# Level products of the last layer's scan: right rows of two tiles packed in one bank, then placed and added by 0/1 products

## What is computed

```python
z = zxbcdt[..., :HID]                       # HID = 512
dt = jax.nn.softplus(dt_raw + dt_bias)
a = (dt * A).reshape(Bsz, nc, Q, H)         # Q = 128 tokens, H = 64 heads
cum = jnp.cumsum(a, axis=2)
diff = cum[:, :, :, None, :] - cum[:, :, None, :, :]
Lmat = jnp.exp(jnp.where(tril, diff, -jnp.inf))
CB = jnp.einsum('bcihn,bcjhn->bcijh', Cc, Bc)
M = CB * Lmat * dtc[:, :, None, :, :]
Yd = jnp.einsum('bcijh,bcjhp->bcihp', M, xs_c)
...
y = (Yd + Yoff).reshape(Bsz, L, H, P) + D[None, None, :, None] * xs
yz = y * (z * jax.nn.sigmoid(z))
yn = yz * rsqrt(mean(yz * yz) + EPS) * norm_w
return yn @ W_out.T
```

## Time and profile before

| | us |
|---|---|
| median of 3 runs | 1101.43 |
| lowest, highest | 1097.45, 1101.68 |
| the profiled execution's own time | 1101.78 |
| its span, first to last instruction | 1100.0 |

### The profile page before, as it was taken

The page is one execution under the profiler, slowest core; times in us unless marked ns, Lnnn a source line. Parts: engine busy times, 40 slices in busy tenths (PEclk is TensorE's granted clock), DMA queues, the critical chain, the costliest instruction groups (busy, mean ns, idle before and its releaser), DMA issues. The chain is left out here.

```text
span 1100.0 us, 12854 instructions
## 1 busy us (share of the span) xinstructions
PE 958.4 (87%) x4126; PEld 497.6 (45%) x4130; DVE 784.6 (71%) x1393; ACT 463.8 (42%) x768; POOL 465.6 (42%) x479
## 2 busy tenths in 40 slices
PE   5998899799999998789999888887888788878887
PEld 2776555233333333445555554344433553364325
DVE  3768465788878886477767457975799469948895
ACT  3332153267666667455554345221621261125311
POOL 2220365554444440263373305930295118710881
PEclk9999699799999999999999978998999899989999
DMA  8500053222222200300000010000000000000000
GB/s 296 205 15 15 15 160 127 68 58 60 59 59 59 59 2 1 136 1 15 15 1 15 1 41 1 1 1 20 0 0 0 20 0 0 0 20 0 0 0 19
DMA packets 28653, 43.11 MB, mean 39 GB/s; under 512 B 6480, under 2 KB 21792, under 8 KB 28192
## 3 DMA queue, kind: packets, MB, share of 16 engines
q1 hardware_dynamic: 28592, 42.41, 12.4%
HBM read 30.93 MB, written 11.27 MB: 38 GB/s over the span
## 5 line engine op out<-in xcount | busy, mean ns | idle before, releaser
L1102 DVE TENSOR_REDUCE l_nmax<-banks 128x1 f32<-128x512 f32 (+1 forms) x165 | 147.8, 930 | 34.9 <-PE banks L1211 33.6
L1057 ACT ACTIVATE l1b_PT<-banks 128x512 f32<-128x512 f32 (+1 forms) x176 | 134.1, 793 | 66.8 <-PE banks L1224 66.4
L2442 PE MATMUL banks<-l_scaled,l_cbm 128*128 128x512 f32 x224 | 126.3, 681 | 39.6 <-POOL l_scaled L2153 21.8
L2153 POOL TENSOR_TENSOR l_scaled<-l_X,l_source 128x512 f32<-128x512 f32 x112 | 134.5, 1226 | 0.0
L2321 DVE TENSOR_TENSOR banks<-banks,l_decay 128x512 f32<-128x512 f32 x128 | 88.1, 691 | 12.4 <-PE banks L2442 8.0
L2442 PEld LDWEIGHTS banks<-l_scaled,l_cbm 128*128 128x128 f32 x224 | 40.9, 207 | 112.1 <-POOL l_scaled L2153 80.4
L1211 PE MATMUL banks<-l_KQ 96*128 96x512 bf16 x240 | 81.3, 392 | 8.5 <-DVE l_nmax L1102 5.6
L2295 DVE TENSOR_TENSOR l_y<-l_y,banks 128x512 f32<-128x512 f32 x128 | 86.7, 677 | 1.9
L1224 PE MATMUL banks<-l_KQ 99*128 99x512 bf16 x256 | 85.2, 386 | 2.9 <-ACT l1b_PT L1057 2.1
L2222 ACT ACTIVATE l_hhi<-l_h 128x512 f16<-128x512 f32 (+1 forms) x24 | 15.1, 630 | 136.2 <-DVE l_h L2334 136.2
L2140 POOL TENSOR_TENSOR l_across<-l_X,l_source 128x512 f32<-128x512 f32 x16 | 17.0, 1074 | 121.9 <-ACT l_X L2208 121.9
(11 more groups left out here) (332 smaller groups left out, 2040.9 us busy)
## 6 DMA issues: line engine op xcount, KB each, us to landing
l_split<-l1a_parts SPq DMA_DIRECT2D x16, 384.0 KB, 3.3
l_KQ<-l_split SPq DMA_DIRECT2D x48, 128.0 KB, 2.9
l_KQ<-l_split SPq DMA_DIRECT2D x16, 192.0 KB, 3.1
l_KQ<-l_split SPq DMA_DIRECT2D x48, 64.0 KB, 2.8
w_ternary<-l_tern_out SPq DMA_DIRECT2D x7, 384.0 KB, 2.3
x<-in_x SPq DMA_DIRECT2D x4, 512.0 KB, 9.5
l_raw<-in_w_gate_up SPq DMA_DIRECT2D x2, 1024.0 KB, 10.1
out<-x SPq DMA_DIRECT2D x4, 512.0 KB, 3.0
```

Source lines behind the costliest of these rows:

```text
L1057: nc.scalar.activation(PT[:, first:first + size, :], source, ACT.Exp, scale=SCALE).then_inc(p_ready, 1)
L1102: nc.vector.tensor_reduce(nmax[:, H % 2, first:first + size], source, axis=AX.X, op=ALU.max, negate=True).then_inc(smax_read, 1)
L2153: nc.gpsimd.tensor_tensor(by_head(scaled[:, n % 4, :]), by_head(X[:, T, :]), spread(source[:, level, T, :]), ALU.mult).then_inc(scaled_rea ...
L2442: last = nc.tensor.matmul(bank, cbm[:, T % 2, level, :], scaled[:, own_n % 4, :], start=True, stop=True)
```

## The change

Only rows of right halves of a level's product are not zero: 64 of 128. The kernel after keeps these rows alone and packs two tiles in one bank.

- `cbm` becomes 128x64 for a level and tile (`right_columns` picks the right tokens' columns). It is made by seven instructions of 64 columns for a tile instead of one of 896, tiles 0 and 1 before the first product and tiles 2 and 3 later.
- A unit is a level of a pair of tiles. Its two products (64 output rows each) go to the lower and upper half of one bank by `tile_position`. There are 14 units and four across products, in `ITEMS`; they take turns in banks 4 and 5.
- DVE decays the whole bank once for a unit and writes the result to `decayed` in SBUF (ring of three). The decays of the packed rows are new: 14 small products with `prefix` and one exponential on ACT (`right_decay`).
- PE places the rows: for each unit two products with 64 source rows and a 128-wide 0/1 matrix (`place`), which add up over the seven levels in bank 6 and bank 7. DVE adds each of these banks to `y` once for a tile (`take_placed`).
- `y` = X times `coef` (`start`) and `hlo` (`rest_of_gated`) move from POOL to DVE. The hidden products stand at other places, the first of them ahead of the first product.
- DVE's order is written out call by call.

```diff
+                    if n == 4:
+                        act.wait_ge(sums_made, b * 3 + 3)
+                        nc.scalar.activation(right_decay[:, :, :, :].rearrange("p l t h -> p (l t h)"),
+                                             k.pair(0).rearrange("p n s -> p (n s)")[:, 0:LEVELS * 2 * L3_HEADS],
+                                             ACT.Exp).then_inc(decay_ready, 1)
...
+                    for level in range(LEVELS):
+                        half = 1 << level
+                        last = nc.vector.tensor_tensor(cbm[:, T, level, :].rearrange("p (b h) -> p b h", h=half),
+                                                       right_columns(diagonal, level),
+                                                       w.masks[:, level, :].rearrange("p (b h) -> p b h", h=half), ALU.mult)
...
+                    if T is None:
+                        u = UNIT.index(n)
+                        if u == 0:
+                            dve.wait_ge(decay_ready, b * 3 + 3)
+                        if u >= 3:
+                            dve.wait_ge(placed, b * OWN + (u - 2))
+                        nc.vector.tensor_tensor(by_head(decayed[:, u % 3, :]), by_head(bank),
+                                                spread(right_decay[:, level, pair, :]), ALU.mult).then_inc(bank_read, 1)
...
+                    nc.vector.tensor_tensor(y[:, T, :], y[:, T, :], ps[6 + T % 2][:, :], ALU.add).then_inc(y_taken, 1)
...
+                take_decayed(5)
+                mask(2)
+                rest_of_gated(1)
+                take_decayed(6)
+                gated(2)
+                mask(3)
+                take_decayed(7)
...
+                take_decayed(14)
+                take_decayed(15)
+                gated(5)
+                take_decayed(16)
+                take_placed(2, 15)
+                weigh(2)
+                rest_of_gated(5)
+                take_decayed(17)
+                take_placed(3, 17)
+                weigh(3)
...
+                pe.wait_ge(decay_ready, b * 3 + 1)
+                for level in range(LEVELS):
+                    for m in range(2):
+                        rows = slice(m * RIGHT, (m + 1) * RIGHT)
+                        columns = slice(level % 4 * 2 * L3_HEADS, (level % 4 + 1) * 2 * L3_HEADS)
+                        last = nc.tensor.matmul(ps[level // 4][rows, columns], w.prefix[:, level, :],
+                                                a[:, m::2, :], start=True, stop=True, tile_position=(0, m * RIGHT))
...
+                        for m in range(2):
+                            rows = slice(m * RIGHT, (m + 1) * RIGHT)
+                            last = nc.tensor.matmul(bank[rows, :], cbm[:, 2 * pair + m, level, :], scaled[:, (2 * u + m) % 4, :],
+                                                    start=True, stop=True, tile_position=(0, m * RIGHT))
...
+                    for m in range(2):
+                        rows = slice(m * RIGHT, (m + 1) * RIGHT)
+                        last = nc.tensor.matmul(ps[6 + m][:, :], w.place[rows, level, :], decayed[rows, u % 3, :],
+                                                start=(level == 0), stop=(level == LEVELS - 1))
...
+                for n in range(NI + 2):
+                    if n < NI:
+                        product(n)
+                        for j in range(FT):
+                            if HIDDEN_AT[j] == n:
+                                hidden(b, j)
+                    if n >= 2 and ITEMS[n - 2][2] is None:
+                        place(n - 2)
```

More of the change, by code:

```diff
@@ L1885, with right_half, right_columns @@
 PREFIX, SUFFIX = LEVELS, LEVELS + 1
+RIGHT = P // 2
+def right_half(level):
+    k, half = np.arange(RIGHT), 1 << level
+    return k // half * 2 * half + half + k % half
+def right_columns(ap, level):
+    return ap.rearrange("p (b two h) -> p b two h", two=2, h=1 << level)[:, :, 1, :]
 def weights3(k, aps, loaded):
@@ L1911, in layout3 @@
     tok = np.arange(P)
-    masks, sums = [], []
+    masks, sums, places = [], [], []
     for level in range(LEVELS):
@@ new lines, in _ @@
+                for u in range(OWN):
+                    pair, level = divmod(u, LEVELS)
+                    for m in range(2):
+                        T = 2 * pair + m
+                        if level == 0:
+                            pool.wait_ge(xtok_ready, b * TT + (T + 1))
+                        if u >= 2:
+                            pool.wait_ge(prod_made, b * NI + (UNIT[u - 2] + 1))
+                        nc.gpsimd.tensor_tensor(by_head(scaled[:, (2 * u + m) % 4, :]), by_head(X[:, T, :]),
@@ L2307, in _, with rest_of_gated @@
+                def rest_of_gated(j):
+                    rows = P if j < FT - 1 else LAST
+                    dve.wait_ge(hhi_ready, b * FT + (j + 1))
+                    nc.vector.tensor_tensor(hlo[0:rows, j, :], h[0:rows, j % 2, :], hhi[0:rows, j, :],
+                                            ALU.subtract).then_inc(hsplit, 1)
+                for T in range(2):
+                    dve.wait_ge(cb_ready, b * TT + (T + 1))
+                    mask(T)
                 dve.wait_ge(cb_ready, b * TT + TT)
@@ new lines, in product, with place @@
+                    last.then_inc(prod_made, 1)
+                def place(n):
+                    pair, level, _ = ITEMS[n]
+                    u = UNIT.index(n)
+                    pe.wait_ge(bank_read, b * NI + (n + 1))
+                    if level == 0:
+                        if pair:
+                            pe.wait_ge(y_taken, b * TT + 2)
+                        else:
+                            pe.wait_ge(cb_ready, b * TT + TT)
+                    for m in range(2):
+                        rows = slice(m * RIGHT, (m + 1) * RIGHT)
+                        last = nc.tensor.matmul(ps[6 + m][:, :], w.place[rows, level, :], decayed[rows, u % 3, :],
+                                                start=(level == 0), stop=(level == LEVELS - 1))
+                    last.then_inc(placed, 1)
```

215 lines of the change are left out of this document (111 added, 104 removed).

## The result

The changed kernel takes 1071.54 us in the median (1070.45 to 1074.18, 4 runs); the kernel before took 1099.47 beside it (1097.45 to 1101.68, 4 runs). The ratio is 0.9755, interval 0.9728 to 0.9783: 28 us faster, where I forecast 22 us slower and my range began at 1089. The profiled execution has a span of 1069.7 us instead of 1100.0.

What follows compares the result with a forecast made beforehand. POOL's instructions were taken to set the pace, DVE hardly behind, both taking turns on two-SBUF instructions. 4.1 + 0.9 + 0.5 = 5.5 us a pass, 22 us for four, gave 1124 us; range 1089 to 1150.

Steps and rivals of the forecast that it cites:

- Ahead of the section: Before each pass's section: 14 prefix products and ACT's exponential add 0.2 to 1.6 us, taken as 0.9 a pass.
- The section: Each pass's section, laid out in time with DVE and POOL taking turns: ends 4.1 us later in a pass.
- rows 6: Trace rows before: `on_diag`, reading two SBUF tiles, takes 0.28 us alone, up to 1.16 beside a running `scaled`.
- Head: Section start: masks delay first product to 794.4 (before 791.50); `coef`, each waiting for a `scaled`, ends 800.4 (before 794.7).
- My layout: Second pass's section put on a clock, DVE and POOL waiting in turns; good to some 4 us a pass.
- Middle: Mid-section: masks of tiles 2 and 3 meet POOL, 811.5 to 817.0 and 818.8 to 823.3; PE stands 820.4 to 824.8.
- End: Section end: last `hlo` ends at 850.0, down products wait for it and start at 850.2 (before 846.05).
- my faster rival: Section: POOL's relief comes through, 3.2 us early less 0.9 for prefix, 2.3 a pass, some 1092 us; chance 0.22.
- the one on TensorE's waits: In the section: right if PE waits mostly for DVE, no longer POOL; wrong if its waits are still on `scaled`.
- Packing: PE in the section: packed products and placings taken at 1.0 us each, between 0.86 (full overlap) and 1.72 (none).
- the rival with 1.7 us: PE's placings or packed products do not overlap: 6 us more a pass, 1148 us; chance 0.14.
- Clock: PE stands three times for 3 to 4.4 us a pass, slowing its clock: 0.5 us a pass (0 to 2).

Runs made afterwards that it cites:

- the short and filled kernel before: Kernel before with one dt series term fewer (shorter VectorE loop body) and three idle TensorE products at the loop's head: 1082.14 us, ratio 0.9844.
- the short kernel before: Kernel before with one dt series term fewer, so a shorter VectorE loop body, and nothing of the change: 1094.31 us, ratio 0.9949.

## Why the prediction was wrong

**Ahead of the section (+0.9 a pass; measured -6.8 to -7.1 in passes 2 to 4).** The step that failed is one that I didn't take: I read no loop head. For this stretch I costed the 14 prefix products and the exponential and took the rest as unchanged. The term itself is 0.0 to 0.1: with loop bodies that fit and an equal clock, the kernel before (less one term of its series) and the changed one both take 32.07 us. The other 20.6 us hung on things that I didn't look at. DVE's loop body went from 278 instructions to 256 and so past the step between 257 and 260; the copy of `xnT` came 3.3 to 3.4 us sooner, three times, 10.1 us. And the clock at the head, 3.4 to 3.6 us three times, 10.5 us. It stood in the trace of before: a copy with 5.05 us of idle time and no releaser, once a pass from the second pass on, and 36 instruction packets on the page. A count of both loop bodies would have shown that the length changes; that 278 is fetched again and 256 isn't, and that the clock would hold, no row of before could tell.

**The section (+4.1; measured -1.2 in the mean).** The mechanism was right, the sizes not. Single instructions in the changed kernel, ns smallest/median/largest:

```profile
L2306 DVE TENSOR_TENSOR l_cbm<-l_cb,w_masks x112: 209/211/1116, 667.6 to 1018.7; 128x64 f32<-128x64 f32 x112
...
L2370 DVE SCALAR_TENSOR_TENSOR l_coef<-l_dt,l_diag,w_heads x16: 280/1106/1109, 673.0 to 999.0; 128x64 f32<-128x64 f32 x16
```

Short ones that meet POOL pay for a whole `scaled`, just as rows 6 had it. What I mis-sized is how often they meet. The second pass's section, timeline of the changed kernel:

```profile
775.13 3.85 DVE L2306 TENSOR_TENSOR l_cbm<-l_cb,w_masks 128x64 f32<-128x64 f32 x14 [3.03 <-ACT l_cb L2226]
...
779.22 1.94 PE L2532 MATMUL banks<-l_scaled,l_cbm 128*64 128x512 f32 x8 [2.28 <-DVE l_cbm L2306]
...
780.54 4.09 DVE L2370 SCALAR_TENSOR_TENSOR l_coef<-l_dt,l_diag,w_heads 128x64 f32<-128x64 f32 x4
784.56 1.27 DVE L2325 TENSOR_TENSOR l_decayed<-banks,l_right_decay 128x512 f32<-128x512 f32 x2
...
796.88 4.01 DVE L2306 TENSOR_TENSOR l_cbm<-l_cb,w_masks 128x64 f32<-128x64 f32 x7
...
802.61 1.02 DVE L2306 TENSOR_TENSOR l_cbm<-l_cb,w_masks 128x64 f32<-128x64 f32 x7
...
805.03 2.56 POOL L2161 TENSOR_TENSOR l_scaled<-l_X,l_source 128x512 f32<-128x512 f32 x2 [4.63 <-PE banks L2532]
```

- Head. I had 4.9 us for the first two masks, it was 3.85; the first product 6.9 us after POOL's start, it was 6.0; the first decay 12.9, it was 11.3 (before: 7.2, by rows 5). The delay is there and 1.6 us smaller. In the third pass it isn't: there `coef` takes 0.87 us and the first decay comes at 8.1.

```profile
889.22 0.87 DVE L2370 SCALAR_TENSOR_TENSOR l_coef<-l_dt,l_diag,w_heads 128x64 f32<-128x64 f32 x4
889.96 4.18 POOL L2161 TENSOR_TENSOR l_scaled<-l_X,l_source 128x512 f32<-128x512 f32 x4 [3.87 <-PE banks L2532]
```

  In both passes DVE comes to `coef` 7.3 us into the section. POOL starts again at 7.2 in the second pass and at 8.1 in the third, because the products that it waits for ran there at a clock of 0.66 (887.9 to 892.9 us) and not 1.00. So slower products made this section the shortest of the four, 56.65 us. It is the same in seven of the sixteen passes of the changed kernel's two profiles and those with one memset and with idle products: 56.5 to 56.7 us with 0.87, 57.4 to 58.5 with 4.1. My layout had no such pass, and nothing that I worked out says which passes get it.
- Middle, the larger error. I gave masks of tiles 2 and 3 together 10.0 us, they took 5.0. "Mask(3) meets three more POOL instructions" was false: POOL had filled its four buffers and stood 4.63 us for TensorE, so seven masks passed in 1.02 us. In my layout POOL was behind what its ring lets it do; here it had done all of it.
- End. The down products start 0.1 us behind the last `hlo`, as forecast, but 58.5 us into the section instead of 62.7.

With POOL's `scaled` waits of TensorE's loads halved (80.4 to 37.5 us) and nothing as large in their place, this is my faster rival at 0.4 to 0.5 of its size: it said 3.2 us less a section, 1.2 were measured in these two profiles; the sections at an undisturbed clock in the kernels with idle products give 58.8 against 57.2, 1.6.

```profile
PEld banks L2532 <- POOL l_scaled L2161: 37.5, 29, 2.9
...
DVE l_decayed L2325 <- PE banks L2532: 27.8, 24, 2.5
```

Of my signs the one on TensorE's waits came half true: its products now waited for DVE longer than for POOL (18.8 against 8.3 us, before 17.2 against 21.8), but its weight loads still name `scaled` first, which I had listed as a sign of being wrong. One sum of the working was off and nothing hangs on it: DVE's terms for a pass before add up to 52.8 us, not about 51.

**Packing.** Right. A packed pair with 64 rows each and the placing behind it start 1.0 us apart, so the halves overlap; the rival with 1.7 us is out.

```profile
789.08 1.08 PE L2532 MATMUL banks<-l_scaled,l_cbm 128*64 128x512 f32 x4
...
790.09 1.13 PE L2553 MATMUL banks<-l_decayed,w_place 64*128 64x512 f32 x4
...
791.15 1.08 PE L2532 MATMUL banks<-l_scaled,l_cbm 128*64 128x512 f32 x4
```

**Clock (+0.5).** Wrong in sign: 0.97 over the second pass's section instead of 0.94:

```profile
773.20:831.80 58.60, 49.60 (x181) 14.95 (x180) 45.99 (x80) 12.95 (x26) 37.33 (x32) 0.97 0.00 0
```

The slow stretch that I feared is there, 0.71 from 784.2 to 790.0 us, but it is the only one of this section; why the kernel before has more slow time in its section isn't shown. Two profiles of kernels with the old section show it falling further, to 0.91 and 62.7 us, which none of the packed ones did.

**What the change itself is worth.** Of 30.3 us of span: 10.1 the loop body, 10.5 the clock at the heads, 4.9 the sections (1.9 of it the lucky third pass), 4.8 layers that it doesn't touch, 0.7 of the first pass, less 0.7 behind the last. The loop body's 10.1 need no packing, as two kernels show. Between the two kernels with idle products and bodies that fit the spans differ by 16.5 us: 10.2 in the sections (4 of them in the disturbed one), 4.3 ahead of layer 3, 2.8 in the first pass, less 0.8 behind the sections.

**Open.** Why the clock holds at the heads of the changed kernel without idle products (nine of nine later heads in three profiles, the one with a single memset more among them) and falls in others whose instructions there and gaps are the same (none held of nine in three of them, one of three in the fourth). So it isn't decided by what the head itself does; it lies further back or in the moment at which a pass begins, and no run here separates the two. Nor do I know why the short and filled kernel before kept 36.4 us in its first pass where the changed one had 33.6.

## What to carry to other kernels

Count the instructions of each engine's loop body, with register additions and bare waits, before and after a change: a first instruction of a loop that stands with no releaser from the second round on, beside instruction packets that grow with the rounds, says that the body is fetched again (the times of the packets in the trace confirm it), and a second semaphore wait on an instruction is an instruction of its own. Look at the clock at each loop head, and try an idle product in TensorE's gaps there before anything else: it cost nothing that I could measure, and the clock held at all twelve later heads in the profiles of the four kernels that had it; six of these are heads where it fell without. Short VectorE instructions cost by how many of them meet GpSimd's, and by whether GpSimd has buffers free at that moment, so follow GpSimd's ring through the section rather than multiply.

## What I had not expected of the hardware

- A VectorE loop body of 257 instructions ran with 20 packets on the instruction queue and a head of 1.12 us; with 260 it was 35 packets and 4.9 to 5.2 us, in each round after the first; with 278, 4.4 to 4.7 us.
- TensorE ran the 314 (before) and 336 (after) instructions of its own loop body without such a stand: at its heads it waits for DVE in both traces. So the step between 257 and 260 is VectorE's, in this place of this program.
- With four memsets more in the changed kernel each later head lost twice: the copy came 3.8 to 4.0 us later, and some 4 us more went in the work behind it, at a clock of 0.50. The half clock doesn't need the stand, though: the short kernel before had it without.
- Half clock at the right place can make a section shorter, 56.65 us instead of 58.54, because it lets short VectorE instructions through ahead of GpSimd's.
- The same head, instruction for instruction, had the full clock in one pass and half in the next of one execution (32.07 and 35.32 us).
